# FFN gate sums: two elementwise steps per tile go from GpSimd to VectorE

## The reference

```python
base1, base3 = xf @ w1.T, xf @ w3.T              # F = 704 columns
def expert_step(acc, p):
    h1 = base1 + xf @ A1.T @ B1.T * LORA_SCALE
    h3 = base3 + xf @ A3.T @ B3.T * LORA_SCALE
    act = silu(h1) * h3
    out = act @ w2.T + act @ A2.T @ B2.T * LORA_SCALE
    return acc + we[:, None] * out, None
```

## Time and profile before

| | us |
|---|---|
| median of 3 runs | 486.38 (485.92 to 487.13) |
| the profiled execution, its time | 486.17 |
| its span in the trace | 484.4 |
| busy: PE, DVE, ACT, POOL | 440.5, 365.4, 350.5, 331.2 |
| mean granted TensorE clock | 0.985 of full |

### The profile page before, as it was taken

The page is one execution under the profiler, slowest core; times in us unless marked ns, Lnnn a source line. Parts: engine busy times, 40 slices in busy tenths (PEclk is TensorE's granted clock), DMA queues, the critical chain, the costliest instruction groups (busy, mean ns, idle before and its releaser), DMA issues.

```text
span 484.4 us, 12249 instructions
## 1 busy us (share of the span) xinstructions
PE 440.5 (91%) x4504; PEld 315.5 (65%) x4504; DVE 365.4 (75%) x1020; ACT 350.5 (72%) x636; POOL 331.2 (68%) x256
## 2 busy tenths in 40 slices
PE   3796989999999999999999997998898896999985
PEld 3372666787878787777788776877664352554553
DVE  3588877889888889888889888988746658533645
ACT  3424999999799989889988889898526556523331
POOL 4125789998769986769999868734227445683573
PEclk9985999999999999999999999999999999999999
DMA  8235342685423674434365414462110000000001
GB/s 295 74 99 186 108 127 72 175 185 171 120 77 87 171 158 126 116 72 127 101 165 154 130 23 110 89 177 45 23 23 0 2 0 1 1 1 0 23 22 45
DMA packets 57276, 44.60 MB, mean 92 GB/s; under 512 B 36608, under 2 KB 48896, under 8 KB 57216
## 3 DMA queue, kind: packets, MB, share of 16 engines
q1 hardware_dynamic: 55728, 41.70, 31.8%
q10 hardware_dynamic: 1488, 2.10, 1.2%
HBM read 23.87 MB, written 11.53 MB: 73 GB/s over the span
## 4 chain that ended last, share of the span: by engine, by line
PE 50%; ACT 14%; issue 13%; POOL 12%; DVE 9%; DMA 1%; POOLq 0%; SPq 0%; ACTq 0%; DVEq 0%
PE ps L482 11%; PE ps L408 7%; PE ps L410 6%; PE ps L409 6%; POOL av_l L1474 5%; PE ps L464 5%; PE ps L466 5%; ACT prob L836 4%; ACT ph L843 3%; POOL gsum L1537 3%; PE ps L502 3%; PE ps L506 3%; PE ps L504 3%; ACT rot L815 2%; DMA wst<-chunks 1%
## 5 line engine op out<-in xcount | busy, mean ns | idle before, releaser
L1149 DVE CUSTOM_DVE_ANT_0 prob<-ps,causal 128x512 f32<-128x512 f32 (+3 forms) x256 | 117.8, 484 | 7.5 <-PE ps L466 5.7
L836 ACT ACTIVATE prob<-prob,least 128x512 f32<-128x512 f32 (+3 forms) x256 | 122.5, 555 | 0.6 <-DVE least L1149 0.5
L1157 DVE SCALAR_TENSOR_TENSOR pl<-ps,ph 128x512 f16<-128x512 f32 (+1 forms) x128 | 105.1, 821 | 22.5 <-ACT ph L843 19.0
L843 ACT ACTIVATE ph<-ps 128x512 f16<-128x512 f32 (+1 forms) x128 | 87.0, 703 | 20.9 <-PE ps L482 18.5
L482 PE MATMUL ps<-ident,prob 128*128 128x128 f32 x640 | 81.6, 274 | 1.9 <-ACT prob L836 1.1
L464 PE MATMUL ps<-kT_h,qT 128*128 128x512 f16 (+3 forms) x256 | 76.5, 301 | 6.9 <-DVE least L1149 3.7
L482 PEld LDWEIGHTS ps<-ident,prob 128*128 128x128 f32 x640 | 68.7, 141 | 3.4 <-DVE pl L1157 2.1
L466 PE MATMUL ps<-kT_l,qT 128*128 128x512 f16 (+3 forms) x256 | 70.1, 301 | 0.0
L502 PE MATMUL ps<-vh,ph 128*128 128x65 f16 x640 | 64.9, 194 | 0.5 <-DVE pl L1157 0.4
L504 PE MATMUL ps<-vl,ph 128*128 128x64 f16 x640 | 64.9, 193 | 0.0
L506 PE MATMUL ps<-vh,pl 128*128 128x65 f16 x640 | 64.8, 193 | 0.0
(11 more groups left out here) (180 smaller groups left out, 1030.0 us busy)
## 6 DMA issues: line engine op xcount, KB each, us to landing
spill<-rot SPq DMA_DIRECT2D x20, 512.0 KB, 3.3
qT<-spill SPq DMA_DIRECT2D x16, 512.0 KB, 3.5
wst<-chunks SPq DMA_DIRECT2D x30, 256.0 KB, 4.1
kT_h<-spill SPq DMA_DIRECT2D x8, 256.0 KB, 3.9
oT<-wmod ACTq DMA_DIRECT2D x3, 512.0 KB, 11.6
kT_l<-spill SPq DMA_DIRECT2D x4, 256.0 KB, 5.4
raw<-chunks SPq DMA_DIRECT2D x4, 256.0 KB, 4.8
out<-xs SPq DMA_DIRECT2D x4, 256.0 KB, 2.2
```

What stands on the lines that cost most here:

```text
L836: act.activation(prob[:, m % 2, c], prob[:, m % 2, c], ACT.Exp, bias=least[:, m % 2, qt:qt + 1], scale=-1.0).then_inc(exp_done, 1)
L843: act.activation(ph[:, m % 2, c], ps[:, PT_BANK:PT_BANK + 3, :].rearrange("p a b -> p (a b)")[:, c], ACT.Copy, scale=PROB_SCALE).then_inc( ...
L1149: ins = dve.tensor_tensor_reduce(prob[:, m % 2, at:at + w], ps[:, bank, off:off + w], causal[:, S - w:S], -1.0 / HD ** 0.5, 3.0e38, ALU.ad ...
L1157: dve.scalar_tensor_tensor(out=pl[:, m % 2, c], in0=ps[:, PT_BANK:PT_BANK + 3, :].rearrange("p a b -> p (a b)")[:, c], scalar=PROB_SCALE, ...
```

## The change

VectorE takes over `sums` and `sums_low`. In its list gsum(i-1) comes behind the first product of tile i, and gsum_l(i-2) behind that; gsum_l(5) is made in tile 6 already (none in tile 7), and behind the last tile come gsum_l(10), the low part of the last product, gsum(11) and gsum_l(11). GpSimd keeps the low parts of the products and of the inputs, in the order in which they stood. What is computed is the same, and so are the waits of each operation.

```diff
@@ VectorE
+            def sums(i):
+                m = min(P, F - i % FT * P)
+                dve.wait_ge(fs["a"], 2 * i + 2)
+                wait(dve, fs["gl"], i - 1)
+                dve.tensor_tensor(gsum[0:m, i % 2, :], av[0:m, i % 2, 0, :], av[0:m, i % 2, 1, :], ALU.add).then_inc(fs["g"], 1)
+
+            def sums_low(i):
+                m = min(P, F - i % FT * P)
+                dve.wait_ge(fs["gh"], i + 1)
+                dve.tensor_tensor(gsum_l[0:m, i % FT, :], gsum[0:m, i % 2, :], gsum_h[0:m, i % FT, :], ALU.subtract)\
+                   .then_inc(fs["gl"], 1)
@@
             for b in range(B):
                 for f in range(FT):
                     activation_product(b, f, 0)
+                    i = b * FT + f
+                    if i > 0:
+                        sums(i - 1)
+                    if i > 1 and i != FT + 1:
+                        sums_low(i - 2)
+                    if i == FT:
+                        sums_low(i - 1)
@@
+            sums_low(B * FT - 2)
             products_low_last()
+            sums(B * FT - 1)
+            sums_low(B * FT - 1)
             lora_sum(1)
@@ GpSimd
-            def sums(i):
...
-            def sums_low(i):
...
             for i in range(B * FT):
                 products_low(i, 0)
-                sums(i)
                 if i < B * FT - 1:
                     products_low(i, 1)
                 if i == 5:
                     difference_low(1)
-                sums_low(i)
                 if i == 2:
                     input_low(1)
```

More of the change, by code:

```diff
@@ L1532, in products_low @@
                 low(av_l[0:m, i % 2, s, :], av[0:m, i % 2, s, :], av_h[0:m, i % 2, s, :], "al")
-            def sums(i):
-                m = min(P, F - i % FT * P)
-                pool.wait_ge(fs["a"], 2 * i + 2)
-                pool.tensor_tensor(gsum[0:m, i % 2, :], av[0:m, i % 2, 0, :], av[0:m, i % 2, 1, :], ALU.add).then_inc(fs["g"], 1)
-            def sums_low(i):
-                m = min(P, F - i % FT * P)
-                pool.wait_ge(fs["gh"], i + 1)
-                low(gsum_l[0:m, i % FT, :], gsum[0:m, i % 2, :], gsum_h[0:m, i % FT, :], "gl")
             for i in range(B * FT):
                 products_low(i, 0)
-                sums(i)
                 if i < B * FT - 1:
```

## The result

| | before | changed |
|---|---|---|
| median, us | 486.51 (14 runs) | 483.31 (14 runs, 480.18 to 485.04) |
| ratio, 95% interval | | 0.9924 [0.9906, 0.9942] |
| profiled execution, us | 486.17 | 482.55 |
| busy: PE, DVE, ACT, POOL | 440.5, 365.4, 350.5, 331.2 | 441.5, 386.5, 350.5, 307.7 |

A forecast was written before the change was run, and what follows sets the result against it. TensorE, working nearly without a pause, was taken to bound the FFN. The terms -2.25 - 1.11 + 0.26 - 1.47 = -4.6 us took 486.17 to 481.6, forecast as a median of 481.7 us; range 480.0 to 484.3.

The forecast's parts named there:

- (a): Tiles 3 and 4, around 400 us: both z stalls go and the third mask transpose comes earlier; -2.25 us.
- (b): Tile 5: masked inputs queue behind gsum_l(3) on VectorE, but are covered with 1.6 us to spare; 0.
- (c): Stalls at 417.57 and 447.94 go, since av_l no longer queues behind gsum and gsum_l; -1.11 us.
- (d): From the stall at 463.14, VectorE leads and takes turns with GpSimd: the stall's 0.71 us is lost, +0.26 us added.
- (e): The end, last pr to first b2 product: VectorE's row of operations takes 8.56 us instead of 10.03; -1.47 us.
- The port: VectorE operations with SBUF inputs wait for GpSimd's current one, at most 1.0 us; GpSimd at most 0.5; queued, they alternate.
- half: Rival: another wait takes over around tiles 3 to 5 and (d) costs 0.9; -2.3 us, 484.1 us; chance 0.17.
- no change: Rival: work moved between users of one port stays on it, z products come as late; 486.4 us; chance 0.05.
- The slower rival: VectorE's queue becomes the bound of every tile and TensorE waits in each; +2.4 us, 488.8 us; chance 0.03.

The follow-up runs named there:

- again: The changed kernel, unedited, traced a second time: this execution took 480.75 us, FFN 124.35 us, no matmul at half clock; median 483.33 us.
- base_first: The changed kernel with the first h matmuls for tile 6 moved in front of the third mask transpose: 480.65 us.
- pad_pause: The changed kernel with eight idle matmuls in TensorE's pause before the third mask transpose: 480.74 us.
- best: The changed kernel with tile 6's first h matmuls before the third mask transpose, gsum_l(3) behind the masked inputs, VectorE's last operations reordered: 479.34 us; repeated, 479.58.
- before_base: The kernel before with only the first h matmuls for tile 6 moved in front of the third mask transpose: 491.39 us.
- tail: The changed kernel with VectorE's last four new operations reordered, gsum(11) straight behind the last av: 482.42 us.
- again2: The changed kernel, unedited, traced a third time: 483.05 us, FFN 127.20 us, twelve matmuls at half clock.
- again3: The changed kernel, unedited, traced a fourth time: 486.25 us, FFN 127.28 us, twelve matmuls at half clock.

## Why the prediction was right, and where its sizes were off

Direction, mechanism and range held; the sum was 4.6 us, and `again`, the trace without a fall of the clock, has 5.1. That the median lay inside the range is in part luck: the fall of the clock had no term, and the room for it in the range was made for other reasons. The steps of `again`, each against the start of its FFN (348.37, which is 0.32 us earlier than before):

| step | row | before | again | forecast | measured |
|---|---|---|---|---|---|
| (a) | third mask transpose | 409.12 | 406.82 | -2.25 | -1.98 |
| (b), (c) | pr(9,1) | 455.36 | 451.93 | -1.11 | -1.13 |
| (d) | pr(11,1) | 468.10 | 463.96 | +0.26 | -0.71 |
| (e) | first b2 product | 478.13 | 472.72 | -1.47 | -1.27 |

**(a)** went as walked. VectorE's timeline of the first trace, against the earlier trace rows:

```profile
400.67 0.68 DVE L1324 TENSOR_TENSOR gsum_l<-gsum,gsum_h 128x512 f16<-128x512 f32 x1
401.27 1.71 DVE L1254 TENSOR_SCALAR wide<-fsm 128x512 f32<-128x512 f32 x2
403.02 0.69 DVE L1257 TENSOR_TENSOR wide<-wide 128x512 f32<-128x512 f32 x1
403.63 0.17 DVE L1263 TENSOR_SCALAR fs<-fs 128x4 f32<-128x4 f32 x1
...
404.27 0.69 DVE L1299 TENSOR_TENSOR pr<-ps,sil 128x512 f32<-128x512 f32 x1
```

The pair is there, GpSimd takes its one turn (the wide masks take 1.71 us instead of 0.8), and pr starts at 404.27; 404.15 was forecast. Counted from the start of the FFN, which the forecast took from the trace before, pr comes at 55.74 us in again (404.11) against 55.46: the 0.3 us that (a) fell short. The port was rightly read, but one row named for it was not: the pr of 406.42 overlaps GpSimd by only 0.05 us. The trace before has a better one, the pr of 398.24, which took 0.69 us beside GpSimd's operation of 398.39. What the working left out is the other side of it: with its two stalls gone TensorE is at the transposes early and stands still there in one piece, 3.18 us in again. **(b)** was covered: in the first trace gsum_l(3) waits 2.46 us for gsum_h(3) and TensorE never waits for the masked inputs; base_first, which takes the cover away, shows the price.

**(d)** is the term with the wrong sign. I let each of the four new operations between av(9,1) and the last pr wait a turn, and carried the lateness into the last tile. In the trace the first two do wait:

```profile
456.42 1.65 DVE L1319 TENSOR_TENSOR gsum<-av 128x512 f32<-128x512 f32 x1
457.99 1.64 DVE L1324 TENSOR_TENSOR gsum_l<-gsum,gsum_h 128x512 f16<-128x512 f32 x1
...
460.88 0.68 DVE L1299 TENSOR_TENSOR pr<-ps,sil 128x512 f32<-128x512 f32 x1
...
463.52 0.67 DVE L1319 TENSOR_TENSOR gsum<-av 128x512 f32<-128x512 f32 x1
464.12 0.68 DVE L1324 TENSOR_TENSOR gsum_l<-gsum,gsum_h 128x512 f16<-128x512 f32 x1
465.79 0.68 DVE L1299 TENSOR_TENSOR pr<-ps,sil 64x512 f32<-64x512 f32 x1 [0.99 <-PE ps L665]
```

In tile 10 both take a turn, and pr(10,1) starts with no idle time before it, so VectorE is just the bound there: it comes 7.12 us after pr(9,1) instead of 6.70, 0.42 later where 0.5 was walked. But in the next tile VectorE's pair runs through with 0.68 us each while GpSimd, which starts at 463.03, is held by all of it: its two low parts take 3.90 us together.

```profile
463.03 3.90 POOL L1496 TENSOR_TENSOR av_l<-av,av_h 128x512 f16<-128x512 f32 x2 [3.94 <-ACT av_h L953]
```

So turns are not strict: here three operations of VectorE that follow straight on each other (av from 462.91, and the pair) went before GpSimd's. Why they do here and not a tile earlier stays open. pr(11,1) then waited 0.99 us for TensorE, and the 0.71 of the stall came through in full. **(e)** was right to 0.2 us.

**What the sum had no term for is the clock.** The rival "half" (484.1) was nearer the median of 483.31 than the forecast, but not for its reason: without a fall (a) gained 1.98 us, not 1.2, and (d) cost nothing; in 19 of 25 executions the time lay above the 480.9 us of the undisturbed group. The rival "no change" fell: of 5.1 us, 2.1 come from moving work between two users of one port. The Trainium skill, "Perfetto Trace Analysis", section "Optimizing Scalar/DVE Operations", warns that it "might not help"; here it does. An operation that took 1.15 to 1.26 us on GpSimd takes 0.68 on VectorE, or 1.65 with its turn: 11 of the 24 were stretched so, nearly half where a third was forecast, and all 24 took 26.8 us instead of 16.5. VectorE's busy time still rose by only 21.1, as its older operations wait less. GpSimd's fell by 23.5 us, not 29, since its av_l now take 33.4 us instead of 28.9. TensorE does not wait for any of it in the second half before the first b2 product (0.6 us). The slower rival stayed away, but its point was near: VectorE's idle time before pr in tiles 8 and 9 fell to 0.6 us, and in tile 10 to none.

## What to carry to other kernels

When an engine is late and idle at once, look at what stands first in its queue and for whom it waits; reordering that list gave 3.0 of the 5.1 us here, and the move to another engine the rest. When stalls are removed, add up where TensorE's pauses now meet: pauses of 1.64, 1.96 and 0.89 us with work between them became one of 3.2 us, and more than half of the executions (15 of 25) lie in the group whose traces show the clock fall behind it. Fill such a pause with later work, or with matmuls into a free bank, and compare executions by their clock before explaining a median.

## What was not expected of the hardware

- The same pause (3.18 us) was followed by full clock in one execution and by twelve matmuls at 1.2 GHz in another; with 1.2 us of it left, none of 18 executions (pad_pause, base_first, best, best_again) went above 481.6 us. The fall of twelve matmuls costs about 2.9 us (127.20 against 124.35).
- Shorter pauses can do it too: in before_base pauses of 1.96 and 1.97 us were followed by four and three matmuls at half clock, while the same 1.96 in the trace before was followed by none.
- A fall also came without such a pause: at 393.6 us, behind the gate product of sixteen matmuls of 8 columns and a pause of 0.34 us, in the first trace of the changed kernel and in that of tail, and in none of the other twelve, which have the same product. It cost at most 0.5 us, as the wait for the masks took it up. Why it came in these two stays open.
- VectorE's operations in a row can keep GpSimd waiting through all of them; GpSimd's two took 3.90 us instead of 2.3.
- The start of the FFN moves by up to 3.1 us between traces of one kernel. Between again2 and again3 it is the transfer of q at the start of the attention (2.59 and 4.53 us of waiting, reached 1.0 us apart); what delays that was not tried.
